# Every second late weight half piece gets its low part from GpSimd instead of VectorE

## What is computed

```
x   = layernorm(x).reshape(T, H)              # T = 2048 tokens, H = 256
w, idx = top_k(softmax(x @ gate_w.T), 2)      # 2 of 8 experts for each token
for gup, dn, ce in experts:                   # 8 of them
    g, u = split(x @ gup.T, 2)                # 1024 wide each
    out += ce[:, None] * (silu(g) * u @ dn.T)
```

## Time and profile before

| | us |
|---|---|
| median of 3 runs (lowest, highest) | 607.62 (602.35, 608.39) |
| profiled execution | 606.88 |
| its span, first to last instruction | 605.2 |
| busy: TensorE matmul | 500.8 (83%) |
| busy: TensorE weight load | 372.3 (62%) |
| busy: VectorE | 394.6 (65%) |
| busy: ScalarE | 349.2 (58%) |
| busy: GpSimd | 272.5 (45%) |
| chain that ended last, share of TensorE / VectorE / DMA / ScalarE / GpSimd | 57% / 13% / 9% / 9% / 3% |

### The profile page before, as it was taken

The page is one execution under the profiler, slowest core; times in us unless marked ns, Lnnn a source line. Parts: engine busy times, 40 slices in busy tenths (PEclk is TensorE's granted clock), DMA queues, the critical chain, the costliest instruction groups (busy, mean ns, idle before and its releaser), DMA issues.

```text
span 605.2 us, 12286 instructions
## 1 busy us (share of the span) xinstructions
PE 500.8 (83%) x3882; PEld 372.3 (62%) x3897; DVE 394.6 (65%) x803; ACT 349.2 (58%) x653; POOL 272.5 (45%) x347
## 2 busy tenths in 40 slices
PE   5667989999998877013888999989999999999980
PEld 3444656766766545002667787768777887777750
DVE  5345568988886554892589888865656656655541
ACT  2211778977887862001797887756566556555540
POOL 4016547556654532003226554654555555644244
PEclk9995899999998885557899999999999999999995
DMA  7558476777585311401257666643243223322223
GB/s 237 183 154 232 150 223 157 232 225 203 170 248 177 125 52 67 126 0 35 76 155 169 161 158 161 164 122 45 53 72 52 55 46 62 53 55 44 27 27 43
DMA packets 57626, 72.55 MB, mean 120 GB/s; under 512 B 18712, under 2 KB 42904, under 8 KB 57432
## 3 DMA queue, kind: packets, MB, share of 16 engines
q1 hardware_dynamic: 46048, 56.03, 30.6%
q0 software_dynamic: 11520, 15.74, 15.4%
HBM read 49.08 MB, written 22.41 MB: 118 GB/s over the span
## 4 chain that ended last, share of the span: by engine, by line
PE 57%; DVE 13%; DMA 9%; ACT 9%; issue 6%; SPq 3%; POOL 3%; ACTq 0%; POOLq 0%; DVEq 0%
PE bank L1274 21%; PE bank L1290 11%; PE bank L1095 4%; PE bank L1141 4%; PE bank L1127 3%; DMA out<-FB,slot_tok 2%; DMA FB<-w 2%; PE bank L1150 2%; PE bank L1245 2%; DVE FB L1038 2%; DVE FB L1034 2%; PE bank L1164 2%; PE bank L1301 2%; PE bank L1176 2%; PE bank L1109 2%
## 5 line engine op out<-in xcount | busy, mean ns | idle before, releaser
L1274 PE MATMUL bank<-FB,WE 128*128 128x0 bf16 x1440 | 188.7, 281 | 1.2 <-ACT FB L745 1.2
L1274 PEld LDWEIGHTS bank<-FB,WE 128*128 x1440 | 137.3, 98 | 30.6 <-issue 2.1
L1034 DVE TENSOR_TENSOR FB<-FB,bank 128x512 f32<-128x512 f32 x120 | 82.4, 687 | 105.3 <-ACT FB L752 104.1
L613 POOL DMA_INDIRECT out<-FB,slot_tok x60 | 95.7, 1596 | 102.6 <-DVE FB L1046 93.8
L752 ACT ACTIVATE FB<-bank 128x512 f32<-128x512 f32 x120 | 71.7, 598 | 101.7 <-PE bank L1274 90.4
L1290 PE MATMUL bank<-FB,WE 128*128 128x0 bf16 x720 | 104.2, 280 | 12.8 <-DVE FB L1038 9.9
L604 POOL DMA_INDIRECT FB<-x_parts,slot_tok x60 | 64.4, 1073 | 99.5 <-PE bank L1245 47.1
L1290 PEld LDWEIGHTS bank<-FB,WE 128*128 x720 | 63.9, 97 | 41.5 <-issue 26.7
L1038 DVE TENSOR_TENSOR FB<-FB 128x512 bf16<-128x512 f32 x120 | 82.3, 686 | 0.0
L539 POOL TENSOR_TENSOR WE<-FB,WE 128x256 bf16<-128x256 f32 x104 | 68.4, 685 | 23.0 <-ACT WE L644 23.0
L758 ACT ACTIVATE FB<-FB 128x512 bf16<-128x512 f32 x120 | 74.9, 624 | 0.2 <-DVE FB L1034 0.2
(11 more groups left out here) (170 smaller groups left out, 649.2 us busy)
## 6 DMA issues: line engine op xcount, KB each, us to landing
FB<-w SPq DMA_DIRECT2D x26, 512.0 KB, 5.4
WE<-w SPq DMA_DIRECT2D x44, 256.0 KB, 3.2
WE<-q_parts SPq DMA_DIRECT2D x32, 200.0 KB
WE<-x SPq DMA_DIRECT2D x16, 256.0 KB, 5.3
q_parts<-FB SPq DMA_DIRECT2D x32, 128.0 KB
x_parts<-WE SPq DMA_DIRECT2D x20, 128.0 KB, 3.8
out<-WE SPq DMA_DIRECT2D x20, 128.0 KB, 5.5
q_parts<-WE SPq DMA_DIRECT2D x16, 128.0 KB
```

Source lines behind the costliest of these rows:

```text
L613: pool.indirect_dma_start(out=out, out_offset=bass.IndirectOffsetOnAxis(ap=slot_tok[:, c:c + 1].bitcast(U32), axis=0), in_=y_sb[c % 2], in ...
L1034: nc.vector.tensor_tensor(hid[k % 2], hid[k % 2], up_bank[k % 2][1][:, :], ALU.mult).then_inc(h_ready, 1)
L1274: ins = nc.tensor.matmul(to, wf[:, bass.ds(at + o, P)], xgT[s % 2][:, 2 * part + kc, :].shape_from_register(long[s % 2]), start=(z == 0), ...
```

## The change

Of the 44 late half pieces the 22 with even j get their low part from GpSimd, in two instructions of 256 columns each, in place of one of 512 on VectorE. GpSimd does one half piece ahead of each pair of its DMAs in a slot: j = 8 s, 8 s + 2, 8 s + 4 and 8 s + 6. VectorE keeps the 22 with odd j, at the steps with odd c. The one semaphore becomes two, one that counts GpSimd's halves and one that counts VectorE's pieces, and SP and TensorE wait for both where they waited for one.

```diff
--- before.py
+++ after.py
@@ -291,7 +291,8 @@
         parked_in = sem("parked_in")
         late_in = [sem(f"late_in{p}") for p in range(LSTG)]
         late_hi = sem("late_hi")
-        late_lo = sem("late_lo")
+        late_lo_pool = sem("late_lo_pool")
+        late_lo_dve = sem("late_lo_dve")
         y_out = [sem(f"y_out{p}") for p in range(2)]
         xg_in = [sem(f"xg_in{p}") for p in range(2)]
 
@@ -364,6 +365,13 @@
             _, o, apart = piece(n)
             return [WE[:, n // NCH, x + at:x + at + CH // 2] for x in (o, o + apart)]
 
+        def late_done(engine, n):
+
+            if (n + 1) // 2 > 0:
+                engine.wait_ge(late_lo_pool, 2 * ((n + 1) // 2))
+            if n // 2 > 0:
+                engine.wait_ge(late_lo_dve, n // 2)
+
         @block.sync
         def _(sp):
             def load_x(b):
@@ -402,8 +410,10 @@
 
             def load_late(j):
                 n, at = LATE[j]
-                if j >= LSTG:
-                    sp.wait_ge(late_lo, j - LSTG + 1)
+                if j >= LSTG and j % 2 == 0:
+                    sp.wait_ge(late_lo_pool, j - LSTG + 2)
+                if j >= LSTG and j % 2 == 1:
+                    sp.wait_ge(late_lo_dve, (j - LSTG + 1) // 2)
                 sp.dma_start(late_stage[j % LSTG], piece(n)[0][:, at:at + CH // 2]).then_inc(late_in[j % LSTG], 16)
 
             def stack_out(dst, r, parts, a, done):
@@ -514,7 +524,7 @@
             for j in range(len(LATE)):
                 load_late(j)
             sp.wait_ge(split_out, 64)
-            sp.wait_ge(late_lo, len(LATE))
+            late_done(sp, len(LATE))
             sp.dma_start(WE[:, E - 1, 2 * W1N:EW], wd).then_inc(parked_in, 16)
 
         @block.gpsimd
@@ -613,18 +623,30 @@
                 pool.indirect_dma_start(out=out, out_offset=bass.IndirectOffsetOnAxis(ap=slot_tok[:, c:c + 1].bitcast(U32), axis=0),
                                         in_=y_sb[c % 2], in_offset=None, compute_op=ALU.add).then_inc(y_out[c % 2], 16)
 
+            def late_lo_part(j):
+                if j < len(LATE):
+                    pool.wait_ge(late_hi, j + 1)
+                    hi, lo = late_parts(j)
+                    for half in range(2):
+                        c = slice(half * CH // 4, (half + 1) * CH // 4)
+                        nc.gpsimd.tensor_tensor(lo[:, c], late_stage[j % LSTG][:, c], hi[:, c], ALU.subtract).then_inc(late_lo_pool, 1)
+
             for c in range(SUB + 2):
                 gather(c)
             for s in range(NS):
+                late_lo_part(FC * s)
                 if s + 1 < NS:
                     gather(SUB * (s + 1) + 2)
                     gather(SUB * (s + 1) + 3)
+                late_lo_part(FC * s + 2)
                 if s > 0:
                     scatter(SUB * (s - 1))
                     scatter(SUB * (s - 1) + 1)
+                late_lo_part(FC * s + 4)
                 if s + 2 < NS:
                     gather(SUB * (s + 2))
                     gather(SUB * (s + 2) + 1)
+                late_lo_part(FC * s + 6)
                 if s > 0:
                     scatter(SUB * (s - 1) + 2)
                     scatter(SUB * (s - 1) + 3)
@@ -1048,7 +1070,7 @@
             def late_lo_part(j):
                 dve.wait_ge(late_hi, j + 1)
                 hi, lo = late_parts(j)
-                nc.vector.tensor_tensor(lo, late_stage[j % LSTG], hi, ALU.subtract).then_inc(late_lo, 1)
+                nc.vector.tensor_tensor(lo, late_stage[j % LSTG], hi, ALU.subtract).then_inc(late_lo_dve, 1)
 
             for s in range(NS):
                 for c in range(FC):
@@ -1056,7 +1078,7 @@
                     hidden(k)
                     if k > 0:
                         hidden_lo(k - 1)
-                    if 2 <= k <= len(LATE) + 1:
+                    if 2 <= k <= len(LATE) + 1 and k % 2 == 1:
                         late_lo_part(k - 2)
                     if c in (4, 7) and s > 0:
                         result(s - 1, c // 7)
@@ -1261,7 +1283,7 @@
                 if c == 0:
                     pe.wait_ge(xgT_ready, 2 * s + 2)
                     if EARLY <= s < E:
-                        pe.wait_ge(late_lo, min((s - EARLY + 1) * 2 * NCH, len(LATE)))
+                        late_done(pe, min((s - EARLY + 1) * 2 * NCH, len(LATE)))
                     if s == E - 1:
                         pe.wait_ge(parked_in, 16)
                 if k >= 2:
```

## The result

| | median, us | lowest to highest | profiled execution | span | granted clock |
|---|---|---|---|---|---|
| before | 607.83 | 602.35 to 611.38 | 606.88 | 605.2 | 0.912 |
| with the change | 610.66 | 606.18 to 617.84 | 610.86 | 609.1 | 0.913 |

Both medians are of 20 runs. The ratio of after to before is **1.0057, with a 95% interval of 1.0031 to 1.0083**: 3.5 us slower by the ratio and 2.8 us by the medians, clear of no change, and well within the 1% that the prediction called the same. One execution with the change, the one of 617.84 us, counts as slow and is left out of the ratio. The median lies 2.1 us above the forecast of 608.6 us, inside its range.

What follows compares the result with a forecast made beforehand. The prediction took the chain of waits, with `hidden_lo` on it 17 times and TensorE taking over at once, as the bound. It summed 606.88 - 0.75 + 1.7 + 0.8 = 608.6 us, range 603.5 to 614.5 us.

Steps and rivals of the forecast that it cites:

- own sign of being wrong: A slot with late pieces changing by over 1 us either way, or ScalarE waiting for a late load.
- net of +1.75 us: Slots 0 to 5: gains of -0.75 us, VectorE-GpSimd meetings +1.7 us and GpSimd's queue +0.8 us taken together.
- other signs: Slots 0 to 5: `hidden_lo` 0.8 to 1.2 us, chain without c = 4 late low parts, GpSimd 15.5 us busy in slot 2.
- Gain at j = 10: Slot 1, c = 4: `result` comes 0.60 us earlier, but `silu(14)` waits for `up(14)`, so 0.15 us gained.
- Gain at j = 42: Slot 5, c = 4: `result`, two scatters and the second's landing all move earlier, so 0.60 us gained.
- `hidden_lo` of c = 3: Slots 0 to 3: GpSimd's second half holds `hidden_lo` up by about 0.12 us each, +0.5 us.
- Late low part at c = 7 of slot 0: GpSimd goes first, VectorE's late low part loses 0.49 us against 0.20 us of slack: +0.3 us.
- `hidden_lo` of c = 7 in slots 1 to 4: GpSimd's pair behind the gathers meets `hidden_lo`: +0.3 us in slot 1, +0.2 us in slots 2 to 4, +0.9 us.
- The queue: GpSimd's fixed order makes the gather used at c = 5 late, 0.6 us in slot 2, 0.2 in slot 3: +0.8 us.
- GpSimd becomes the bound: Rival: GpSimd's pairs lose 0.5 us each, slots 1 to 5 grow, +7 us, 614 us; chance 0.12.
- VectorE loses the port at every `hidden_lo` on the chain: Rival: 17 meetings on the chain of 0.49 us each, 8.3 us, 615 us; chance 0.08.
- The relief is worth more: Rival: meetings cost nothing, both even chain pieces give 0.60 us, a scatter falls better, 604.0 us; chance 0.15.

Runs made afterwards that it cites:

- Experiment 1: Kernel before, VectorE keeping all 44 pieces, plus GpSimd's subtractions on other data at the same places: 617.09 us, ratio 1.0178.
- experiment 3: Kernel before without VectorE's even late low parts; GpSimd does nothing instead, SP fills their places from memory: 608.07 us, ratio 1.0044.
- experiment 7: The change, but GpSimd takes only nine pieces in front of `result` (c = 4, c = 7, from slot 1): 603.39 and 603.58 us, ratios to before 0.9939 and 0.9966.
- Experiment 4: The change with each GpSimd piece as one instruction of 512 columns in place of two of 256: 613.12 us, ratio 1.0115.
- experiment 5: The change with GpSimd's order altered so each pair of gathers comes ahead of the subtractions: 614.33 us, ratio 1.016.
- experiments 5 and 6: The sixth is experiment 5 with GpSimd waiting, before its four subtractions, for VectorE's late piece of c = 3: 609.06 us, ratio 1.0059.

## Why the prediction came out as it did

The forecast of the same was right, and its time was within 2.1 us. By its own sign of being wrong, a slot with late pieces that changes by over 1 us, it failed in slot 2, which grew by 2.7 us; the sum came out near because the other slots moved by 0.5 us at most. The net of +1.75 us was under half of what slots 0 to 5 show (+3.9). Of the other signs, `hidden_lo` at 0.8 to 1.25 us, `hidden` unchanged and the chain without late low parts at c = 4 came true; GpSimd's subtractions (median 0.734 us, up to 1.728, in place of 0.67 and 1.1) and its busy time in slot 2 (19.05 us in place of 15.5) show that it was stopped far more than I had priced.

One row was misread: the 15.21 us that the prediction gives as VectorE's busy time in slot 2 are TensorE's weight loads; VectorE's are 16.48 us. The conclusion (slot 6 is hardly shorter with VectorE busy 11.79 us) does not rest on the difference.

Term by term:

- **Gain at j = 10, -0.15 us.** Right in kind and size: steps c = 4 to 6 of slot 1 took 7.04 us before and 6.95 after, with 0.1 us of the next term but one inside. TensorE takes over, as said.
- **Gain at j = 42, -0.60 us.** The relief came (c = 4 of slot 5 fell from 2.59 to 2.01 us), and the second scatter's issue began 14.31 us after the slot's start, against 14.35 before: so all of it was eaten by c = 0 (+0.16, below) and c = 3 (+0.41) of the same slot. For the 0.41 us no row shows a cause. Net 0.
- **`hidden_lo` of c = 3, +0.5 us** (it runs in step c = 4). Right. GpSimd's start at 316.80 us, not 316.5, was late by as much as VectorE's was, and `hidden_lo` took 0.80, 0.78, 0.89 and 0.80 us in slots 0 to 3, so 0.1 to 0.2 us each: the rest of the running half and then 0.55 us of its own. Steps c = 4 and 5 of slot 3 together are 0.12 us longer.
- **Late low part at c = 7 of slot 0, +0.3 us.** Right: 0.28 us in both executions.
- **`hidden_lo` of c = 7 in slots 1 to 4, +0.9 us** (in step c = 0 of the next slot). Near: 0.25 us in slot 2, nothing in 3, 0.18 in 4 and 0.16 in 5, together 0.6 us.
- **Late low part at c = 7 of slot 2, not in the sum.** 1.36 us in one execution, 0.47 in the other, 0.9 us in the mean. The prediction gave this meeting a place in slot 0 only, and gave one meeting an upper end of 0.5 us, from the attention stage. That bound was a mistake: in the earlier trace rows VectorE met *one* running subtraction. In slot 2 the queue had moved GpSimd's pair, behind two late gathers, onto VectorE's late low part, and VectorE lost the whole row of instructions.
- **The queue, +0.8 us.** The right mechanism, mis-sized: this term is the one that failed. I let a pair take 1.5 us; behind the DMAs each took 1.77 to 1.83. The gather went out 2.7 us later than before in place of 2.15, and TensorE waited 0.89 us. Steps c = 4 and 5 of slot 2 together grew from 4.68 to 5.95 and 6.42 us; less the 0.2 us of `hidden_lo` in them that is 1.1 to 1.5 us. Slot 4 gave 0.3 us more [the landing at 377.11 us], slot 3, for which I had 0.2, nothing. Together 1.4 to 1.9 us.

The two that were off, 0.8 us of the queue and 0.9 us of the late low part, are most of the 2 us between the net and the stage. In slot 2 they are one event: a GpSimd queue that has no gap left. In slot 4 the same queue makes the gather 2.5 us late, but the slot is 1 us longer and TensorE loses 0.3 us.

**The rivals.** *GpSimd becomes the bound* had its condition met for slots 1 and 2 (pairs lose 0.5 us), and the gather was late beyond its slack, but the queue did not stay full: in the first half of slot 3 GpSimd waited for `result` and for high parts again, its first two pairs took 1.30 us, and where it filled up again (360.54 to 377.11 us) slot 4 took most of it in, so 614 us didn't come. *VectorE loses the port at every `hidden_lo` on the chain* was further off than it looked for a reason I hadn't seen: the change takes its even late low parts away from VectorE, and those would have been what collides. Experiment 1, where they stay, lost 10.8 us, an estimated 2.8 of it to the clock. *The relief is worth more* finds no support in experiment 3, as far as that shows it (c = 4). Its core is true of the nine pieces that experiment 7 moves.

By the Trainium skill (SBUF — State Buffer, "SBUF: two separate sides"), of a VectorE instruction with two inputs in SBUF and a GpSimd instruction that reads SBUF, the one that starts first holds the shared ports to its end. Experiment 4 agrees: a `hidden_lo` stands up to 2.25 us beside one subtraction of 1.16 us, and up to 1.25 us beside two of 0.67. The row of 3.35 us in experiment 5 goes beyond what that page states, since four instructions went ahead of one.

**Open:** when VectorE loses a whole row of subtractions and when it gets in between. At 346.20 us its instruction had begun 0.16 us before the end of a gather's issue that had subtractions behind it, and lost them all; three such cases in experiment 5 and four in experiment 4 went the same way. At 307.09 us it had begun 0.12 us after the start of a subtraction, with the issue 0.26 us past, and got in. But two `hidden_lo` in experiment 1 that had begun 0.28 us before the end of a gather's issue, and one in experiment 5 that had begun 0.44 us before it, went ahead (0.85, 0.87 and 1.06 us). And at c = 1 in experiments 5 and 6 a late low part that had begun about 0.8 us before the end of a scatter's issue stood through the rest of it and one subtraction of the two, 2.05 to 2.17 us in all. So the rows give a pattern with exceptions, and no experiment set the offset. Open too: why the clock fell in four of the 14 profiles (at the start of slot 6, and in experiment 1 in slot 2 as well), the 1 to 3 us of experiment 7 beyond its slots, and the 0.41 us at c = 3 of slot 5.

## What to carry to other kernels

Move to GpSimd only the work that the chain of waits names: here nine of 44 pieces, chosen by it, made the kernel faster, and every second piece made it slower. Count a GpSimd subtraction twice, once in its own queue, for the gathers behind it, and once in every two-input VectorE instruction that it meets. Price the meeting by the longest row of GpSimd instructions that can stand ready there, not by one, and if VectorE's piece must come first, make GpSimd wait for it. Before comparing two times by a few us, compare their granted clocks.

## What the runs showed of the hardware that I had not expected

- A two-input VectorE instruction of 0.68 us stood for 2.04 us through two GpSimd subtractions of 256 columns, 3.35 us through four, and up to 2.25 us beside one of 512 columns; where a half was just running it took the rest of that half and 0.55 us, 0.80 to 1.16 us.
- An instruction with one operand in PSUM (`hidden`) kept to 0.69 us everywhere, and GpSimd's fills, which only write, left VectorE's late low parts at 0.677 to 0.705 us (88 in two executions).
- GpSimd pays in return: a pair takes 1.30 us alone and 1.8 us where it meets one VectorE instruction.
- After TensorE had been busy for 0.41 of 2.4 us, waiting twice for a gather, its granted clock stood at the 1.2 GHz level for 6.9 us (experiment 1, slot 2): a late gather cost more than the wait for it.
